# A one-core decoder layer: the scatter of finished rows behind the turn of the probabilities, and a prologue with x by partition, small weights first and aggregations inside the scale chains

## The chip, the cores and the metric

The kernel runs on one core of one Trainium2 chip. The metric is the device time of one execution in microseconds (us). A core has a matmul engine (TensorE, PE in the rows), a vector engine (VectorE, DVE), an activation engine (ScalarE, ACT), a general engine (GpSimd, POOL) and a queue engine for transfers (SyncE, SP). Each engine works through its own instructions in the order in which they are written; semaphores tie the engines together.

## The reference

x is 128 sequences of 64 tokens of 128 numbers; ctx has the same shape. Three residual blocks follow one another:

```
x = x + attention(layernorm(x))                 # 16 heads of 8, one key and value head
x = x + xattn(layernorm(x), ctx)                # a recurrence over the 64 tokens
x = x + ffn(layernorm(x))                       # 8 experts, top 1, 128 -> 512 -> 128

def step(carry, x_t):                           # xattn, for all 128 sequences
    h0, c0 = lstm_cell(concat(x_t, a), h0, c0, Wi0, Wh0, bi0, bh0)
    h1, c1 = lstm_cell(h0, h1, c1, Wi1, Wh1, bi1, bh1)
    attn  = softmax(einsum('bh,bsh->bs', h1 @ Wq.T, context))
    mixed = einsum('bs,bsh->bh', attn, context)
    a     = tanh(concat(mixed, h1) @ Wo.T + bo)
```

The outputs a of the recurrence are the second block's outputs. Each of its 64 steps needs the one before.

## The kernel before

The program has four stages, each a block with code of its own for every engine.

**Prologue** (lines 175 to 380). x is loaded in 8 chunks and ctx in 4 (SP's queue), the weights by ACT's queue. DVE takes the statistics of 64 token tiles of x (`bn_stats`, L293), aggregates them (`bn_aggr`, L296), takes the largest magnitudes of the weights and of ctx (L300 to L317) and makes scales that are powers of two from them (L319 to L343; the last of them releases `v_scale`). Numbers are kept as a high and a low 16-bit part: ACT makes the high parts of the 20 blocks of LSTM weights (`WL`, L212), and ACT and DVE the two parts of the projected context (`KH`, `VH`, L219 to L372) from TensorE's products (L278, L283), in 16 chunks through two buffers each (c % 2), so that chunk c waits until DVE has taken chunk c - 2. POOL makes the LSTM's bias rows (L254 to L262).

**Self-attention** (L483 to L775). 64 token tiles pass through a software pipeline, step i for tile i. Its result is `yv` (L756, DVE). POOL normalises tiles (L522, L528), adds `yv` to x (L534), and in steps 2 to 11 makes the low parts of the LSTM weights (`weight_rest`, L489 and L492, two blocks a step), which only the recurrence reads.

**Recurrence** (L985 to L1475). The 128 sequences are two groups of 64, a (G[0]) and b (G[1]), that run half a step apart. `half(L, A, ...)` is half a step: group L is in its LSTM cells while group A is in its cross-attention. It is called with L = a, A = b (the odd half) and then with L = b, A = a (the even half). The chain through one half on engine A's side is: scores (PE L1076) of the new hidden state, masked by DVE into `sm` (L1427), row maximum `nm` (L1433), exponent (ACT L1167), normalised probabilities `pe` (DVE L1444), their transpose by TensorE, the turn (L1108, semaphore `s_pt`), their two halves `pmv` (DVE L1454, L1456), the mixing matmuls `mx` (PE L1126), their sum `ar` (L1467), tanh on ACT (L1194) and the two parts of the new output `a_a` or `a_b` (DVE L1471, L1473). On L's side stand two LSTM cells: gates on PE (L1003), `gt` on ACT, `u`, `c` and `h` on DVE (L1393 to L1413).

Beside it runs a side line for tokens that are finished: `add_x1` (residual, L1334), statistics (L1339, L1343), `rstd` (POOL, L1246 to L1255), `normalise` (DVE L1350, writes `XN`), `copy_xn` (POOL L1281, L1282, into the row in `TOK`), router logits and the choice of an expert, `place` (POOL L1261 to L1268, a row's place) and `scatter` (POOL L1275): an indirect DMA that writes 128 rows of 258 numbers into `sorted_x` at the places in `slot`. One scatter stands in each odd half from step 4 on: 60 of them, and four more behind the last step. `TOK` has four slots, so that `add_x1` of token t waits for the landing of the scatter of token t - 4. What POOL runs in an odd half is written so:

```
if odd == 1 and live(t - 4):
    place(t - 4, (m - 4) % SLOTS)
    scatter(t - 4, (m - 4) % SLOTS)
if L:
    pool.tensor_copy(L.xs[:, :, :], XTn(L, lt + 1)).then_inc(L.s_xs, 1)
if odd == 1 and live(t - 1):
    rstd(t - 1)
```

**Experts** (from L1540): tiles of 128 sorted rows are read back, go through their expert's two layers and are scattered to the output.

## Time and profile before

| | |
|---|---|
| time, median of 3 runs | 1565.74 us (1564.30 to 1566.23) |
| time of the profiled execution | 1570.4 us |
| its span | 1568.7 us |
| prologue | 0 to 83 us |
| self-attention | 83 to 405 us |
| copying and start of the recurrence | 405 to 442 us |
| recurrence | 442 to 1377 us |
| tables, then experts | 1377 to 1398, then to 1568.7 us |
| busy: PE, DVE, ACT, POOL | 85%, 69%, 47%, 38% of the span |

The profile is of one execution. The rows that are shown further down give a start or a total in us, an engine, a line of the kernel, an operation with what it writes and reads, and in brackets how long the engine was idle ahead of it and what released it.

### The profile page before, as it was taken

The numbers are of one execution on the slowest core, as the hardware profiler recorded it, in microseconds if no ns is written. First come the engines' busy times: TensorE is split into PE (matmuls) and PEld (weight loads), VectorE is DVE, ScalarE is ACT, GpSimd is POOL, SyncE is SP. The second block draws the span as 40 slices with busy tenths as digits, with TensorE's granted clock in tenths as the row PEclk, the third lists the DMA queues.
The fourth block names the chain that finished last, engine by engine and source line by source line (L and its number), as shares of the span: only waits on it lengthen the run. The fifth ranks groups of instructions, "written<-read, shape, count | busy, mean of one in ns | idle before, by whom it ended". The sixth has DMA issues, their size and how long they took to land. (4 is left out here: it accounts for less than half of the span.)

```text
span 1568.7 us, 83724 instructions
## 1 busy us (share of the span) xinstructions
PE 1335.8 (85%) x34523; PEld 1195.8 (76%) x34523; DVE 1089.8 (69%) x4580; ACT 742.8 (47%) x2203; POOL 599.5 (38%) x1485
## 2 busy tenths in 40 slices
PE   0867888888499999999999999999999999839997
PEld 0556666666388888888888888888888888729996
DVE  7778999999456666666666666666666666636664
ACT  0656777787234444444444444444444444315553
POOL 1337555555402333333333333333333333224444
PEclk9979999999699999999999999999999999959999
DMA  8000000000320000000000000000000000022332
GB/s 255 1 2 16 17 17 17 17 17 17 110 53 11 19 16 18 19 16 18 19 16 18 19 16 18 19 16 18 19 16 18 19 16 18 14 82 80 95 96 56
DMA packets 49055, 52.62 MB, mean 34 GB/s; under 512 B 6026, under 2 KB 42252, under 8 KB 48168
## 3 DMA queue, kind: packets, MB, share of 16 engines
q1 hardware_dynamic: 41040, 32.50, 7.4%
q0 software_dynamic: 5344, 12.66, 2.3%
q8 instruction: 275, 4.51, 1.2%
q10 hardware_dynamic: 2296, 2.14, 0.4%
q14 instruction: 100, 0.82, 0.2%
HBM read 28.31 MB, written 19.42 MB: 30 GB/s over the span
## 5 line engine op out<-in xcount | busy, mean ns | idle before, releaser
L1076 PE MATMUL sc_ab<-h_a,KH 128*128 128x48 f16 (+2 forms) x4096 | 123.2, 183 | 2.2 <-DVE h_a L1413 2.2
L1076 PE MATMUL sc_ab<-h_b,KH 128*128 128x48 f16 (+2 forms) x4096 | 123.4, 183 | 0.3 <-issue 0.2
L1149 ACT ACTIVATE gt_a<-z_a,sc 128x256 f32<-128x256 f32 x128 | 60.6, 474 | 128.9 <-PE z_a L1003 128.9
L1126 PEld LDWEIGHTS mx_ab<-pmv_b,VH 128*128 128x128 f16 x4096 | 107.1, 96 | 16.3 <-DVE pmv_b L1456 16.3
L1126 PE MATMUL mx_ab<-pmv_b,VH 128*128 128x16 f16 x4096 | 113.0, 169 | 5.3 <-DVE pmv_b L1456 0.4
L1003 PE MATMUL z_a<-h_a,WL 128*128 128x64 f16 x2304 | 112.4, 193 | 5.6 <-DVE h_a L1405 2.0
L1003 PE MATMUL z_b<-h_b,WL 128*128 128x64 f16 x2304 | 112.0, 193 | 5.6 <-DVE h_b L1405 0.4
L1076 PEld LDWEIGHTS sc_ab<-h_a,KH 128*128 128x128 f16 x4096 | 113.1, 96 | 2.3 <-DVE h_a L1413 2.3
L1076 PEld LDWEIGHTS sc_ab<-h_b,KH 128*128 128x128 f16 x4096 | 113.3, 96 | 0.7 <-issue 0.5
L1126 PE MATMUL mx_ab<-pmv_a,VH 128*128 128x16 f16 x4096 | 112.2, 169 | 0.4 <-DVE pmv_a L1456 0.2
L1149 ACT ACTIVATE gt_b<-z_b,sc 128x256 f32<-128x256 f32 x128 | 60.6, 473 | 107.0 <-PE z_b L1003 107.0
L1589 POOL DMA_INDIRECT out<-ys,xr x71 | 70.2, 989 | 102.8 <-DVE ys L1689 80.0
L1126 PEld LDWEIGHTS mx_ab<-pmv_a,VH 128*128 128x128 f16 x4096 | 108.1, 96 | 1.0 <-DVE pmv_a L1456 1.0
L1261 POOL TENSOR_TENSOR w<-lr,one 128x8 f32<-128x8 f32 x60 | 12.1, 202 | 237.3 <-ACT lr L1189 237.3
L1003 PEld LDWEIGHTS z_a<-h_a,WL 128*128 128x128 f16 x2304 | 84.9, 97 | 19.8 <-DVE h_a L1413 10.4
L1650 ACT ACTIVATE hT<-psHa,b_sb 128x128 f32<-128x128 f32 x213 | 62.7, 365 | 75.0 <-PE psY L1622 38.9
L1003 PEld LDWEIGHTS z_b<-h_b,WL 128*128 128x128 f16 x2304 | 84.5, 97 | 17.4 <-DVE h_b L1413 12.9
L649 ACT ACTIVATE prT<-psT 128x512 f32<-128x512 f32 x128 | 69.9, 595 | 54.6 <-PE psT L585 54.6
L585 PE MATMUL psT<-ident,pr 128*128 128x128 f32 x512 | 73.5, 289 | 21.2 <-ACT pr L671 20.9
L1275 POOL DMA_INDIRECT sorted_x<-TOK,slot x64 | 70.1, 1096 | 51.1 <-DVE a_a L1473 44.9
L1160 ACT ACTIVATE tc_a<-c_a 128x64 f32<-128x64 f32 x128 | 32.8, 256 | 117.7 <-DVE c_a L1398 117.7
L1246 POOL TENSOR_SCALAR ve<-mvt 128x1 f32<-128x1 f32 x64 | 19.0, 297 | 174.1 <-DVE mvt L1343 174.1
(295 smaller groups left out, 3847.9 us busy)
## 6 DMA issues: line engine op xcount, KB each, us to landing
xr<-sorted_x SPq DMA_DIRECT2D x71, 129.0 KB
X<-in_x SPq DMA_DIRECT2D x8, 512.0 KB, 8.2
XT<-in_ctxT SPq DMA_DIRECT2D x4, 1024.0 KB
x_scratch<-X SPq DMA_DIRECT2D x8, 512.0 KB, 3.2
x1r<-x_scratch SPq DMA_DIRECT2D x64, 64.0 KB, 1.9
X<-in_w SPq DMA_DIRECT2D x1, 2048.0 KB, 9.0
sorted_x<-zt SPq DMA_DIRECT2D x12, 129.0 KB, 3.7
out<-ys,xr POOLq DMA_INDIRECT x71
```

The costliest lines, as they stand in the source:

```text
L585: mm = nc.tensor.transpose(psT[:, hp // 4, (hp % 4) * P:(hp % 4 + 1) * P], pr[:, u, 2 * hp:2 * hp + 2, :].rearrange("p h k -> p (h k)"), i ...
L649: nc.scalar.activation(prT[:, 4 * k:4 * k + 4, :].rearrange("p n t -> p (n t)"), psT[:, k, :], ACT.Copy).then_inc(a_pt, 1)
L1003: mm = nc.tensor.matmul(q.z[layer][:, j * GB:(j + 1) * GB], WL[:, blk + j, w, :], mov[m], start=False, stop=False, skip_group_check=True)
L1076: mm = nc.tensor.matmul(A.S[:, WIDE * n:WIDE * n + streamed(n)], KH[:, k, pair * P:(pair + 1) * P], A.h[1][:, 2 * n:2 * n + streamed(n) // ...
L1126: mm = nc.tensor.matmul(A.M[:, WIDE * n:WIDE * (n + 1)], VH[:, k, pair, :], A.pm[:, 2 * n:2 * n + WIDE // 2, :].rearrange("p b k -> p (b k)"),
L1149: nc.scalar.activation(L.gt[l][:, :, :].rearrange("p g b -> p (g b)"), L.z[l][:, 0:4 * GB], ACT.Tanh, scale=sc[:, I0 + l:I0 + l + 1]).then ...
L1160: nc.scalar.activation(L.tc[l][:, :], L.c[l][:, :], ACT.Tanh, scale=0.5).then_inc(L.s_tc[l], 1)
L1246: pool.tensor_scalar(ve[:, :], mv[:, 1:2], EPS, None, ALU.add).then_inc(g_r, 1)
L1261: pool.tensor_tensor(w8[:, :], lr[:, 1, :], one[:, :], ALU.mult).then_inc(g_pl, 1)
L1275: pool.indirect_dma_start(xs_dram, bass.IndirectOffsetOnAxis(slot[:, u:u + 1], 0), TOK[:, u, :], None).then_inc(d_sc[u], 16)
L1589: pool.indirect_dma_start(out_rows, bass.IndirectOffsetOnAxis(xr[:, u, AT_ROW:].bitcast(U32), 0), ys[:, u % 4, :], None, bounds_check=last ...
L1650: ins = nc.scalar.activation(hT[:, u, c, :], psHa[:, u, c * P:(c + 1) * P], ACT.Relu, bias=b1_sb[:, bass.ds(e * FC + c, 1)])
```

## The change

It has three parts.

**In the recurrence**, POOL's scatter moves behind the copy `xs` of the same odd half and gets one more wait, for the turn of group b's probabilities (`s_pt`). The wait is TensorE's transpose L1108. DVE's `normalise` moves from the even half's start to a place behind the second cell's `c`. `place` stays where it was.

**In the prologue**, x comes as `xP`, laid out on the host so that each partition reads 4 KB in one piece for a chunk and not 512 B rows; ACT's queue issues the six small weight loads ahead of the LSTM weights and biases; masks are made first on DVE; half of the 64 aggregations stand between the statistics and the other half inside two scale chains (`meanwhile`); the first chain covers the weights alone and releases ACT's `WL` copies and POOL's biases (`v_scale_w`), the second ctx (`v_scale`); the square root and the reciprocal of the statistics are done in two halves, the second of them, `WO2`'s low part and `smask` at the prologue's end.

**The low parts of the LSTM weights** (`weight_rest`) move from the attention steps 2 to 11 to the end of POOL's prologue.

```
 # recurrence, POOL
                         if odd == 1 and live(t - 4):
                             if not isinstance(t, int) or t < T:
                                 place(t - 4, (m - 4) % SLOTS)
-                            scatter(t - 4, (m - 4) % SLOTS)
                         if L:
                             if not (isinstance(lt, int) and lt == T - 1):
 
                                 ready(L.s_ah, 2 * lt)
                                 pool.wait_ge(L.s_xu, lt + 1)
                                 pool.tensor_copy(L.xs[:, :, :], XTn(L, lt + 1)).then_inc(L.s_xs, 1)
+                        if odd == 1 and live(t - 4):
+                            if A:
+                                pool.wait_ge(A.s_pt, at + 1)
+                            scatter(t - 4, (m - 4) % SLOTS)
 # recurrence, DVE
                         if odd == 0:
-                            if live(t - 2):
-                                normalise(t - 2, (m - 2) % SLOTS)
                             if live(t - 4):
                                 gate(t - 4, (m - 4) % SLOTS)
...
                         if L:
                             cell(1)
+                        if odd == 0 and live(t - 2):
+                            normalise(t - 2, (m - 2) % SLOTS)
 # self-attention, POOL
                     def step(i, u):
-                        if 2 <= i < 12:
-                            weight_rest(2 * i - 4)
-                            weight_rest(2 * i - 3)
 # prologue, POOL
-                    pool.wait_ge(v_scale, 1)
+                    pool.wait_ge(v_scale_w, 1)
...
+                    for blk in range(20):
+                        col = (S0 if blk < 12 else S1) + (8 if blk % 4 == 2 else 0)
+                        pool.wait_ge(a_w, blk + 1)
+                        if blk > 0:
+                            pool.wait_ge(g_wl, 2 * blk)
+                        pool.tensor_scalar(wlt[:, :], wl32[:, blk * P:(blk + 1) * P], sc[:, col:col + 1], None,
+                                           ALU.mult).then_inc(g_wl, 1)
+                        pool.wait_ge(g_wl, 2 * blk + 1)
+                        pool.tensor_tensor(WL[:, blk, 1, :], wlt[:, :], WL[:, blk, 0, :], ALU.subtract).then_inc(g_wl, 1)
 # prologue, SP
-                        sync.dma_start(Xp[:, k * nx:(k + 1) * nx, :], xw[:, k * nx:(k + 1) * nx, :]).then_inc(s_x[k], 16)
+                        cols = slice(k * nx * D, (k + 1) * nx * D)
+                        sync.dma_start(X[:, cols], xP[:, cols]).then_inc(s_x[k], 16)
 # prologue, ACT
-                    act.wait_ge(v_scale, 1)
+                    act.wait_ge(v_scale_w, 1)
                     for blk in range(20):
                         col = (S0 if blk < 12 else S1) + (8 if blk % 4 == 2 else 0)
                         nc.scalar.activation(WL[:, blk, 0, :], wl32[:, blk * P:(blk + 1) * P], ACT.Copy,
                                              scale=sc[:, col:col + 1]).then_inc(a_w, 1)
+                    act.wait_ge(v_scale, 1)
 # prologue, DVE (the new order)
+                    for k in range(XCH):
+                        dve.wait_ge(s_x[k], 16)
+                        for n in range(k * nx, (k + 1) * nx):
+                            nc.vector.bn_stats(st6[:, n, :], Xp[:, n, :]).then_inc(v_st, 1)
+                        if k < XCH // 2:
+                            for n in range(k * nx, (k + 1) * nx):
+                                aggregate(n)
+                    variance(0)
...
+                    def spread(k):
+
+                        meanwhile(6)
+                        dve.wait_ge(p_sc, 2 * k + 1)
+                        nc.vector.tensor_reduce(mxr[:, :], psS[0:8, 0:P], AX.X, ALU.max).then_inc(v_rd, 1)
+                        dve.wait_ge(v_rd, 2 * k + 1)
+                        nc.vector.tensor_scalar(dg[:, :], ident[0:8, 0:8], mxr[:, 0:1], None, ALU.mult).then_inc(v_rd, 1)
+                        meanwhile(5)
+                        dve.wait_ge(p_sc, 2 * k + 2)
+                        step(nc.vector.tensor_scalar(gm[:, :], psS[:, 128:136], 1e-12, 1e12, ALU.max, ALU.min))
+                    spread(0)
```

On POOL, in the odd half of a step in the middle of the recurrence, the order before is this (`slot` and `acc` end `place`; the DMA is the scatter; `ve` begins `rstd`):

```order
L1267 TENSOR_SCALAR slot<-w2s 128x1
L1268 TENSOR_TENSOR acc<-acc,one 128x8
L1275 DMA sorted_x<-TOK,slot 67584x258
L1295 COPY xs_a<-XT 128x128
L1246 TENSOR_SCALAR ve<-mvt 128x1
L1248 TENSOR_TENSOR yr<-ve,mhalf 128x1
```

and after the change the same place reads:

```order
L1309 TENSOR_SCALAR slot<-w2s 128x1
L1310 TENSOR_TENSOR acc<-acc,one 128x8
L1336 COPY xs_a<-XT 128x128
L1317 DMA sorted_x<-TOK,slot 67584x258
L1288 TENSOR_SCALAR ve<-mvt 128x1
L1290 TENSOR_TENSOR yr<-ve,mhalf 128x1
```

The scatter and the copy have changed places, and `rstd` now stands directly behind the scatter. On DVE, where an odd half ends and an even half begins, before:

```order
L1467 TENSOR_REDUCE ar_b<-mx_ab 128x64
L1471 TENSOR_SCALAR a_b<-a 128x64
L1473 SCALAR_TENSOR_TENSOR a_b<-a,a_b 128x64
L1350 TENSOR_SCALAR XN<-TOK,mvt,rst 128x128
L1385 RECIPROCAL TOK<-smt 128x1
L1427 TENSOR_TENSOR sm_a<-sc_ab,smask 128x128
```

and after the change, at the second cell of the even half:

```order
L1438 SCALAR_TENSOR_TENSOR u_b<-gt_b,c_b 128x64
L1440 SCALAR_TENSOR_TENSOR u_b<-gt_b 128x64
L1443 SCALAR_TENSOR_TENSOR c_b<-u_b 128x64
L1395 TENSOR_SCALAR XN<-TOK,mvt,rst 128x128
L1450 TENSOR_TENSOR h_b<-os_b,tc_b 128x64
```

`XN`, the normalised row, has moved from behind `a_b` to between `c_b` and `h_b` of the same even half.

## Rows read from the trace of the kernel before

**Rows 1.** Waits of VectorE in the recurrence, 500 to 1300 us: total us, times, longest

```profile
DVE sm_b L1427 <- PE sc_ab L1076: 71.7, 55, 1.4
```

**Rows 2.** Timeline of one odd half with a scatter: start us, us, engine, line, operation

```profile
999.03 0.23 DVE L1473 SCALAR_TENSOR_TENSOR a_a<-a,a_a 128x64 f16<-128x64 f32 x1
...
999.45 0.55 PE L1076 MATMUL sc_ab<-h_b,KH 128*128 128x48 f16 x16
...
999.97 0.52 PE L1003 MATMUL z_b<-h_b,WL 128*128 128x64 f16 x12
...
999.54 1.10 POOL L1275 DMA_INDIRECT sorted_x<-TOK,slot  x1 [0.76 <-DVE a_a L1473]
...
1000.92 0.29 DVE L1427 TENSOR_TENSOR sm_b<-sc_ab,smask 128x128 f32<-128x128 f32 x1 [1.33 <-PE sc_ab L1076]
...
1006.83 0.23 DVE L1473 SCALAR_TENSOR_TENSOR a_b<-a,a_b 128x64 f16<-128x64 f32 x1
...
1013.80 0.23 DVE L1473 SCALAR_TENSOR_TENSOR a_a<-a,a_a 128x64 f16<-128x64 f32 x1
```

**Rows 3.** Timeline of VectorE, an odd half of the first steps, without a scatter

```profile
485.38 0.29 DVE L1427 TENSOR_TENSOR sm_b<-sc_ab,smask 128x128 f32<-128x128 f32 x1 [0.45 <-PE sc_ab L1076]
```

**Rows 4.** Timeline, the rest of that odd half: turn, mixing, rstd, next even half

```profile
1003.06 0.33 PE L1108 MATMUL sc_ab<-ident,pe_b 128*128 128x128 f32 x1
...
1003.99 1.76 PE L1126 MATMUL mx_ab<-pmv_b,VH 128*128 128x16 f16 x64
...
1005.79 0.29 DVE L1467 TENSOR_REDUCE ar_b<-mx_ab 128x64 f32<-128x128 f32 x1 [0.40 <-PE mx_ab L1126]
...
1006.26 0.19 POOL L1255 TENSOR_TENSOR rst<-yr,yu 128x1 f32<-128x1 f32 x1 [0.18 <-POOL yu L1253]
...
1009.88 0.28 DVE L1334 TENSOR_TENSOR TOK<-psE,x1r 128x128 f32<-128x128 f32 x1
...
1011.72 0.24 DVE L1405 TENSOR_TENSOR h_b<-os_b,tc_b 128x64 f16<-128x64 f32 x1 [0.32 <-ACT tc_b L1160]
```

**Rows 5.** DMA issues, 1000 to 1100 us: count, median us from issue to landing

```profile
sorted_x<-TOK,slot POOLq DMA_INDIRECT x7, 2.8
```

**Rows 6.** Timeline of VectorE, self-attention: yv of steps 5, 11 and 31

```profile
129.03 0.29 DVE L756 TENSOR_TENSOR yv<-psSc,rden 128x128 f32<-128x128 f32 x1
...
165.19 0.29 DVE L756 TENSOR_TENSOR yv<-psSc,rden 128x128 f32<-128x128 f32 x1
...
257.97 0.29 DVE L756 TENSOR_TENSOR yv<-psSc,rden 128x128 f32<-128x128 f32 x1
```

**Rows 7.** Groups of instructions of GpSimd, 83 to 200 us: busy us, mean ns

```profile
L489 POOL TENSOR_SCALAR wlt<-wl,sc 128x128 f32<-128x128 f32 x20 | 12.1, 603 | 1.0
...
L492 POOL TENSOR_TENSOR WL<-wlt,WL 128x128 f16<-128x128 f32 x20 | 8.5, 427 | 1.7
```

**Rows 8.** Timeline of VectorE in the prologue

```profile
24.60 4.30 DVE L296 BATCH_NORM_AGGREGATE mv<-st 128x2 f32<-128x6 f32 x64
...
45.30 0.17 DVE L343 TENSOR_SCALAR sc<-sc 128x2 f32<-128x2 f32 x1
...
51.78 0.87 DVE L363 SCALAR_TENSOR_TENSOR WO<-wo_sb,sc,WO 128x128 f16<-128x128 f32 x1 [4.57 <-ACT WO L214]
```

**Rows 9.** Timeline of ScalarE, TensorE and GpSimd in the prologue

```profile
45.51 5.95 ACT L212 ACTIVATE WL<-wl,sc 128x128 f16<-128x128 f32 x20 [16.09 <-DVE sc L343]
...
43.39 2.08 PE L278 MATMUL psA<-XT,xwq_sb 128*128 128x512 f32 x2
...
53.37 2.08 PE L278 MATMUL psA<-XT,xwq_sb 128*128 128x512 f32 x2 [3.83 <-DVE KH L368]
...
59.49 1.02 PE L278 MATMUL psA<-XT,xwq_sb 128*128 128x512 f32 x2
...
61.24 1.02 PE L278 MATMUL psA<-XT,xwq_sb 128*128 128x512 f32 x2
...
58.06 1.03 POOL L260 COPY BL<-bhi 1x1024 bf16<-1x1024 bf16 x1
```

More of the change, by code:

```diff
@@ L1 @@
+import itertools
 from contextlib import ExitStack
@@ L224, in _ @@
                                              scale=sc[:, SV:SV + 1]).then_inc(a_v, 1)
+                    act.wait_ge(v_sd, 2)
+                    nc.scalar.activation(sd[:, hp:], sd[:, hp:], ACT.Sqrt).then_inc(a_sd, 1)
                 @block.gpsimd
@@ L267, in _ @@
                     pe.wait_ge(s_const, 8)
-                    pe.wait_ge(v_mx, 8 + CCH)
-                    nc.tensor.transpose(psS[0:8, 0:P], mx[:, :], ident[:, :]).then_inc(p_sc, 1)
-                    pe.wait_ge(v_sc, 2)
-                    nc.tensor.matmul(psS[:, 128:136], ones[0:8, :], dg[:, :], start=True, stop=True).then_inc(p_sc, 1)
+                    for k, m in enumerate((mx, mxb)):
+                        pe.wait_ge(v_mx, (7, 8 + CCH)[k])
+                        wait(pe, v_scale_w, k)
+                        nc.tensor.transpose(psS[0:8, 0:P], m[:, :], ident[:, :]).then_inc(p_sc, 1)
+                        pe.wait_ge(v_rd, 2 * k + 2)
+                        nc.tensor.matmul(psS[:, 128:136], ones[0:8, :], dg[:, :], start=True, stop=True).then_inc(p_sc, 1)
                     pe.wait_ge(s_wo, 96)
@@ L289, in _ @@
                 def _(dve):
-                    for n in range(NPAIR):
-                        if n % (NPAIR // XCH) == 0:
-                            dve.wait_ge(s_x[n // (NPAIR // XCH)], 16)
-                        nc.vector.bn_stats(st6[:, n, :], Xp[:, n, :]).then_inc(v_st, 1)
-                    for n in range(NPAIR):
-                        dve.wait_ge(v_st, n + 1)
-                        nc.vector.bn_aggr(mv[:, n, :], st6[:, n, :]).then_inc(v_st, 1)
-                    dve.wait_ge(v_st, 2 * NPAIR)
@@ L311, in _, with meanwhile, step @@
                                                 apply_absolute_value=True).then_inc(v_mx, 1)
+                    n = 0
+                    rest = iter(range(hp, NPAIR))
+                    def meanwhile(count):
+                        for pair in itertools.islice(rest, count):
+                            aggregate(pair)
+                    def step(ins):
+                        nonlocal n
+                        n += 1
+                        ins.then_inc(v_sc, 1)
+                        meanwhile(1)
+                        dve.wait_ge(v_sc, n)
+                    def spread(k):
[8 more added lines that the diff above has]
+                    spread(0)
+                    step(nc.vector.tensor_scalar(pw[:, :].bitcast(I32), gm[:, :].bitcast(I32), 0x7F800000, None,
+                                                 ALU.bitwise_and))
+                    step(nc.vector.tensor_scalar(tmp[:, 0:2], pw[:, 0:2], 2.0 ** -13, None, ALU.mult))
+                    step(nc.vector.reciprocal(sc[:, 0:2], tmp[:, 0:2]))
+                    step(nc.vector.tensor_scalar(sc[:, 8:10], sc[:, 0:2], 2.0, None, ALU.mult))
+                    nc.vector.tensor_scalar(sc[:, 4:6], tmp[:, 0:2], 0.5 / S, None, ALU.mult).then_inc(v_scale_w, 1)
                     for k in range(CCH):
@@ L366, in _ @@
+                    step(nc.vector.tensor_tensor(tmpb[:, 1:2], tmpb[:, 5:6], pw[:, 3:4], ALU.mult))
+                    step(nc.vector.reciprocal(sc[:, 2:4], tmpb[:, 0:2]))
+                    nc.vector.tensor_scalar(sc[:, 6:8], tmpb[:, 0:2], 1.0 / S, None, ALU.mult).then_inc(v_scale, 1)
+                    dve.wait_ge(a_sd, 1)
+                    nc.vector.reciprocal(rs[:, 0:hp], sd[:, 0:hp]).then_inc(v_rs, 1)
+                    meanwhile(hp)
+                    variance(1)
                     for c in range(16):
@@ L375, in _ @@
                             ALU.mult, ALU.subtract).then_inc(v_v, 1)
+                    dve.wait_ge(a_w, 21)
+                    nc.vector.scalar_tensor_tensor(WO2[:, 1, :], wo_sb[:, 1, :], sc[:, SV:SV + 1], WO2[:, 0, :],
+                                                   ALU.mult, ALU.subtract).then_inc(v_w, 1)
+                    dve.wait_ge(v_pm, 1)
+                    dve.wait_ge(v_scale, 1)
+                    nc.vector.tensor_scalar(
+                        smask[:, :].rearrange("p (n h k) -> p n h k", h=2, k=2),
+                        pm[:, :].unsqueeze(1).unsqueeze(3).broadcast_to([P, GP, 2, 2]),
+                        sc[:, IK:IK + 1], None, ALU.mult).then_inc(v_b, 1)
+                    dve.wait_ge(a_sd, 2)
+                    nc.vector.reciprocal(rs[:, hp:], sd[:, hp:]).then_inc(v_rs, 1)
         clear_semaphores()
```

102 lines of the change are left out of this document (42 added, 60 removed).

## The prediction

> **What bounds the kernel now.** I read three views. The waits of VectorE come first, over 800 us of the recurrence, since that stage is 935 of the 1568.7 us. One line stands out: the mask of group b, `sm_b`, waits 1.3 us at a time for the scores, 71.7 us in 55 waits [rows 1]. The timeline says why that is odd. The scores' last matmuls end at 999.45 + 0.55 = 1000.00, yet `sm_b` starts at 1000.92 [rows 2]; in the first steps, where no token is finished and no scatter runs, the same wait is 0.45 [rows 3]. What lies between is POOL's scatter, 999.54 to 1000.64, and `sm_b` comes 0.28 behind its end. TensorE itself isn't stopped, since its next matmuls run at 999.97 [rows 2]. So the result of a matmul that ends while the scatter runs reaches the engine that waits for it only about 1.38 after the scatter's start (1000.92 - 999.54). The chain of one half passes through this wait: `a_a` 999.03 to `a_b` 1006.83 is 7.80, and the even half without a scatter, to `a_a` at 1013.80, is 6.97 [rows 2]. Difference 0.83, in 60 halves 49.8 us. The longest rows of POOL in self-attention [rows 7] and the prologue's rows [rows 8, 9] give the other two stages.
>
> **The recurrence.** Removed: the scatter beside the scores of b, 60 x 0.83 = **-49.8 us**. Whether it comes back depends on what is awaited from TensorE at the new place. The scatter is now released by the turn, which ends at 1003.06 + 0.33 = 1003.39 [rows 4]. Its row starts some time behind its release; in the present place 0.76 behind POOL's last operation [rows 2]. I take 0.9, since the new release is a semaphore from another engine, so a start at 1004.3 and an end at 1005.4. By the 1.38 the results are held until 1005.68. The result awaited next from TensorE is the mixing product: its matmuls end at 1003.99 + 1.76 = 1005.75, and `ar_b` starts at 1005.79 [rows 4]. The hold is over 0.1 before. It is thin, so I put +0.05 a half, 60 x 0.05 = **+3.0 us**, with bounds of 0 and of the whole 0.83 (49.8 us) if the hold returns.
>
> What else moves with it: behind the scatter in POOL's queue stands `rstd`, six small operations that end at 1006.26 + 0.19 [rows 4]. It waits for the scatter now and ends some 1.6 later, at 1008.1. Its only reader is `normalise`, which therefore would be late at its old place (directly behind `a_b`, 1006.83) and is moved to about 1011.4, where `h_b` waits 0.32 for ACT anyway [rows 4]. A 128x128 operation of some 0.3 fits there: cost 0, at most 0.1 x 60 = 6 us if not. The gain of its removal behind `a_b` is nothing, since `sm_a` waits for the scores there. The scatter's landing, 2.8 after issue [rows 5], now comes at 1004.3 + 2.8 = 1007.1; it must be there for `add_x1` at 1009.88 [rows 4]. The copy `xs` ahead of it comes 1.1 earlier and is awaited by nobody sooner. Recurrence in sum: -49.8 + 3.0 = **-46.8**.
>
> **The Trainium skill against this reading.** The rows show a wait for TensorE that is 0.9 longer with a scatter than without [rows 1, 3]. The Trainium skill (SBUF — State Buffer, section Who interferes with whom) says that "PE and ACT never wait on anyone" and that only the port pair shared by VectorE and GpSimd is contended. By it no result of TensorE could be held, the 0.83 would belong to VectorE's own operations beside a GpSimd instruction and would travel with the scatter; the sum would be that of the rival "it travels" below.
>
> **Self-attention.** `yv` takes 36.16 us from step 5 to step 11 (129.03 to 165.19), and from step 11 to step 31 92.78 us, 4.64 a step [rows 6]. Six steps at 4.64 are 27.8, so the six are 8.3 too long. They are among those in which POOL makes the low parts, 20 pairs of 0.60 + 0.43 us, 20.6 busy [rows 7], most of them in this stretch. With these gone the steps should fall to 4.64. I take **-8.1** (a remainder of a step in its filling), bounds -8.3 and -6.5 (if part of it is a slower clock while the pipeline fills).
>
> **The prologue.** Ahead of the scales now: aggregations 4.30 us in one piece [rows 8], behind statistics that wait for x. With half of them in the load's gaps, half in the chains' gaps, and x in 4 KB pieces, the statistics end at about 22.2 rather than 28.9 (the end of the aggregations, 24.60 + 4.30), so -6.7. A second chain adds about +2.8 (two round trips to TensorE and some six small operations). The scale for ctx, written at 45.30 [rows 8], comes at 45.5 - 3.9 = 41.6. More is gained behind it: ACT makes the 20 weight blocks first, 5.95 us from 45.51 [rows 9], and only then begins on KH, so that TensorE, having filled both buffers, waits 3.83 and begins chunk 2 at 53.37 with matmuls at half speed (2.08 against 1.02 for the same two) [rows 9]. After the change those blocks are done while DVE is in ctx. TensorE starts chunk 0 about 3.8 earlier (43.39 to 39.6) at half speed, some 6.2 for two chunks, and goes on without a pause, each chunk 61.24 - 59.49 = 1.75 [rows 9]: chunk 2 at 46.0, chunk 4 at 49.6 against 59.49, so **-9.8**. Twelve chunks follow at the same rate. At the end DVE has `WO2`'s low part (0.87, [rows 8]), `smask` and a reciprocal that stood earlier; part of it lies behind chunk 15: **+0.9**, bounds 0 and 2. Sum **-8.9**, bounds -5 (x no faster, the aggregations still in the way) and -11.
>
> The low parts cost nothing there as long as POOL is ready first. Its biases took from 45.5 to 59.1 (58.06 + 1.03 [rows 9]), 13.6. They begin at about 29.1 now and end at 42.7; 20 pairs of 1.03 and gaps, 1.22 each, are 24.4, so 67.1. The prologue ends at about 83 - 8.9 = 74: cover 7 us.
>
> **Sum.** -46.8 - 8.1 - 8.9 = -63.8. The profiled execution took 1570.4 (span 1568.7), 4.7 above the median. It would take 1506.6; of the median of 1565.7 it leaves **1501.9**.
>
> **The rivals.**
>
> *The hold catches the mixing product in part.* For it: only 0.1 lies between. If the scatter's row starts 0.3 to 0.7 later than 1004.3 (the lag behind a semaphore is not shown in the middle of the chain), results come free at 1006.0 to 1006.4, `ar_b` is 0.2 to 0.6 late, and 60 x 0.4 = 24 us of the gain go: about 1523. Chance 0.16.
>
> *It travels.* Every scatter costs its half about 0.83 wherever it stands, as contention of VectorE or as a hold that reaches whatever is next. Against it: TensorE's end and the late `sm_b` [rows 2]. At the new place h_a's operations on VectorE would be drawn out, or `ar_b`. Then only prologue and attention remain: 1565.7 - 17.0 = 1548.7. Chance 0.09.
>
> *Slower.* The scatter's start falls at the mixing product's end: then `ar_b` waits the whole 1.38, more than the 0.83 removed. The point at which this outweighs everything is a new hold of (49.8 + 17.0) / 60 = 1.11 a half, that is a scatter that starts behind 1005.79 + 1.11 - 1.38 = 1005.5, 1.2 later than I put it, and ahead of 1005.75. At 1005.7 the hold is 1.29: 77.4 us, and 1565.7 - 17.0 + 77.4 - 49.8 = 1576.3. Chance 0.03.
>
> *POOL ends the prologue.* If the biases and low parts are drawn out by over 7 us, each further us is one. Doubling the pairs' 24.4 would cost 17: 1519. Against it: their durations beside a busy VectorE are in rows 7 already. Chance 0.03.
>
> **How the numbers follow.** The forecast as summed 0.67, its own range 1494 to 1509 (prologue -11 to -5, attention to -6.5, residue 0 to 0.1 a half). In part 0.16, it travels 0.09, POOL last 0.03, slower 0.03, no change 0.02. The range for 8 in 10 reaches from 1492 into the partial case, 1526. Within 0.2% (3 us, about what a measurement tells from no change) needs the gains of prologue and attention to be eaten: 0.02. Faster 0.95, slower 0.03.
>
> **What would show it.** In the changed trace: halves of 6.95 to 7.05 in both parities; `sm_b` waits of 0.45; the scatter's row at about 0.9 behind the turn's end, and the wait of `ar_b` still near 0.40. `normalise` between `c_b` and `h_b` without moving `h_b`. `yv` every 4.64 from the start. The prologue's end at 74, chunk 4 at 49.6, POOL's last low part at 67. The prediction is wrong if the wait of `ar_b` grows beyond 0.5, if `h_a` is late in halves with a scatter, or if DVE still waits for x at 25.

## The result, and the profile after

The changed kernel took 1547.49 us (median of 4 runs, 1544.14 to 1549.10) against 1565.99 for the kernel before on the same chip: a ratio of 0.987, 95% interval 0.985 to 0.989. It is faster, by 18.5 us, where 63.8 were forecast. The profiled execution has a span of 1546.9 us, 21.8 under that of before. By stage, from the traces: self-attention begins at 80.7 instead of 83.1 (-2.5), its steps 5 to 11 give -8.4, the recurrence's first `a_a` comes at 429.34 instead of 442.71 (-13.4 in all up to there), the recurrence from that `a_a` to the last `a_b` takes 925.99 instead of 933.28 (-7.3), and what follows -1.1. Of the 13.4, 2.5 that nobody forecast lie in the other attention steps and in the recurrence's start.

So self-attention did what was forecast, the prologue gave about a quarter of its 8.9, and the recurrence 7.3 of 46.8. These are VectorE's waits in the recurrence, 500 to 1300 us, after the change (total us, times, longest):

```profile
DVE sm_a L1470 <- PE sc_ab L1118: 53.6, 55, 1.8
DVE ar_b L1512 <- PE mx_ab L1168: 39.7, 55, 0.8
...
DVE sm_b L1470 <- PE sc_ab L1118: 25.3, 55, 0.7
```

The wait of `sm_b`, 71.7 in [rows 1], is down to 25.3, as forecast. In its place `ar_b` waits 0.7 for the mixing product at each scatter, and `sm_a`, in the half behind it, up to 1.8. In most even halves `sm_a` itself isn't late (it starts 1.01 behind `a_b` as before); VectorE only waits longer there, since `XN` no longer runs ahead of it. The timeline of one odd half with a scatter shows the first of these:

```profile
1024.77 0.23 DVE L1518 SCALAR_TENSOR_TENSOR a_a<-a,a_a 128x64 f16<-128x64 f32 x1
...
1027.94 0.33 PE L1150 MATMUL sc_ab<-ident,pe_b 128*128 128x128 f32 x1
...
1028.87 1.34 PE L1168 MATMUL mx_ab<-pmv_b,VH 128*128 128x16 f16 x47
...
1029.14 1.09 POOL L1317 DMA_INDIRECT sorted_x<-TOK,slot  x1 [3.54 <-DVE mvt L1388]
...
1030.42 0.59 PE L1168 MATMUL mx_ab<-pmv_b,VH 128*128 128x16 f16 x17 [0.21 <-issue]
...
1031.05 0.29 DVE L1512 TENSOR_REDUCE ar_b<-mx_ab 128x64 f32<-128x128 f32 x1 [0.70 <-PE mx_ab L1168]
...
1032.11 0.23 DVE L1518 SCALAR_TENSOR_TENSOR a_b<-a,a_b 128x64 f16<-128x64 f32 x1
```

The scatter starts 0.87 behind the turn's end (1028.27) and 4.37 behind `a_a`, where it was expected. The mixing matmuls, one piece of 64 in [rows 4], are in two: TensorE stops after 47 of them and goes on at 1030.42, 1.28 behind the scatter's start, and the row names no engine that it waited for ("issue"). The half takes 7.34 instead of 7.80. In all 60 odd halves with a scatter the mixing takes 2.06 to 2.25, where it took 1.76 to 1.87 before, and 59 show such a pause; their median is 7.35, in sum 442.0 us against 466.8, so -24.8.

The even halves took most of it back. 48 of 63 are 6.94 to 7.00 as before, but 15 take 8.05 to 8.21, together +17.5 us. One of them begins at 1046.43, and this is TensorE's clock in stretches of 0.4 us around it (the column behind the busy times is the granted clock; the first row holds the end of the pause, the last one the end of the slow stretch), then the scores in it:

```profile
1044.40:1044.80 0.40, 0.17 (x7) 0.08 (x4) 0.23 (x1) 0.04 (x1) 0.32 (x2) 1.00 0.00 0
1044.80:1045.20 0.40, 0.40 (x18) 0.40 (x18) 0.00 (x0) 0.00 (x0) 0.22 (x2) 0.81 0.27 103
1045.20:1045.60 0.40, 0.40 (x16) 0.40 (x14) 0.23 (x1) 0.00 (x0) 0.40 (x1) 0.50 0.64 228
...
1048.40:1048.80 0.40, 0.40 (x19) 0.40 (x16) 0.28 (x2) 0.28 (x2) 0.00 (x0) 0.92 0.00 0
```

```profile
1045.19 2.08 PE L1118 MATMUL sc_ab<-h_a,KH 128*128 128x48 f16 x48
```

The clock falls to its lower level (0.50, 1.2 GHz) about 0.3 us behind the pause in the mixing matmuls and stays there until 1048.4; the 48 score matmuls take 2.08, against 1.36 at full clock in the half of 1030.87. In the trace of before no even half is long.

The prologue after the change, on VectorE:

```profile
20.21 0.15 DVE L334 TENSOR_SCALAR sd<-mv 128x32 f32<-128x32 f32 x1
27.97 1.75 DVE L346 TENSOR_REDUCE mx<-wl 128x1 f32<-128x1536 f32 x1 [7.61 <-DMA wl<-in_wh1T]
...
44.39 1.71 DVE L378 TENSOR_SCALAR dg<-ident,mxr 8x8 f32<-8x8 f32 x1
```

and on GpSimd and TensorE:

```profile
43.96 2.12 POOL L275 TENSOR_TENSOR bw<-bw,bhi 128x1024 f32<-128x1024 f32 x1
...
52.76 1.02 PE L302 MATMUL psA<-XT,xwq_sb 128*128 128x512 f32 x2
```

The statistics are done at 20.3, earlier than the 22.2 of the forecast. But VectorE then waits 7.61 us for the LSTM weights. Chunk 2 starts at 52.76 against 53.37 [rows 9] and against 46.0 forecast; its clock is the full one, as forecast. A second loss is in `dg`, an 8x8 operation of 0.22 us elsewhere that took 1.71 and ended at 46.10, just behind POOL's operation (43.96 + 2.12 = 46.08). The Trainium skill (SBUF — State Buffer, section Who interferes with whom) has this: a `tensor_scalar` can use the port pair that VectorE shares with GpSimd, and the later one then waits for the whole of the other's instruction. The trace agrees: `dg` started second, at 44.39, and ended with the other.

Self-attention, `yv` of steps 5, 11 and 31:

```profile
126.19 0.29 DVE L798 TENSOR_TENSOR yv<-psSc,rden 128x128 f32<-128x128 f32 x1
...
153.93 0.29 DVE L798 TENSOR_TENSOR yv<-psSc,rden 128x128 f32<-128x128 f32 x1
...
246.74 0.29 DVE L798 TENSOR_TENSOR yv<-psSc,rden 128x128 f32<-128x128 f32 x1
```

Steps 5 to 11 take 27.74, against 36.16 in [rows 6]: -8.4, forecast -8.1.

### The profile page after: what moved, and what is told of

It is laid out like the page before. It is cut to its first block and busy times, and to the rows that moved or that the text cites. A ratio compares the mean times of both kernels' runs of the same rounds, so it can differ in the third digit from the quotient of the medians.

```text
span 1546.9 us, 83762 instructions
## 1 busy us (share of the span) xinstructions
PE 1345.5 (87%) x34526; PEld 1209.5 (78%) x34526; DVE 1102.6 (71%) x4589; ACT 744.3 (48%) x2204; POOL 594.7 (38%) x1485
## 5 line engine op out<-in xcount | busy, mean ns | idle before, releaser
L1168 PE MATMUL mx_ab<-pmv_b,VH 128*128 128x16 f16 x4096 | 122.5, 170 | 19.4 <-issue 14.1
L1168 PEld LDWEIGHTS mx_ab<-pmv_b,VH 128*128 128x128 f16 x4096 | 111.4, 96 | 35.7 <-issue 19.2
L1118 PE MATMUL sc_ab<-h_a,KH 128*128 128x48 f16 (+2 forms) x4096 | 136.2, 189 | 2.2 <-DVE h_a L1458 2.2
L1118 PEld LDWEIGHTS sc_ab<-h_a,KH 128*128 128x128 f16 x4096 | 126.2, 101 | 2.3 <-DVE h_a L1458 2.3
L1323 POOL COPY TOK<-XN 128x128 f32<-128x128 f32 x64 | 18.7, 293 | 260.4 <-DVE XN L1395 260.4
L627 PEld LDWEIGHTS psT<-ident,pr 128*128 128x128 f32 x512 | 55.6, 142 | 34.3 <-ACT pr L713 34.3
L789 DVE TENSOR_REDUCE pmx<-psSc 128x16 f32<-128x1024 f32 x64 | 78.4, 1224 | 3.3 <-PE psSc L618 2.4
```

The costliest lines, as they stand in the source:

```text
L627: mm = nc.tensor.transpose(psT[:, hp // 4, (hp % 4) * P:(hp % 4 + 1) * P], pr[:, u, 2 * hp:2 * hp + 2, :].rearrange("p h k -> p (h k)"), i ...
L789: nc.vector.tensor_reduce(mxv, sv, AX.X, ALU.max).then_inc(v_m, 1)
L1118: mm = nc.tensor.matmul(A.S[:, WIDE * n:WIDE * n + streamed(n)], KH[:, k, pair * P:(pair + 1) * P], A.h[1][:, 2 * n:2 * n + streamed(n) // ...
L1168: mm = nc.tensor.matmul(A.M[:, WIDE * n:WIDE * (n + 1)], VH[:, k, pair, :], A.pm[:, 2 * n:2 * n + WIDE // 2, :].rearrange("p b k -> p (b k)"),
```

## The experiments

The experiments fell on four chips, and the first thing that they showed is that chips are of two kinds. Two of the four behave like that of the result: a result of TensorE that falls due beside a scatter is held back from the engine that waits for it. This is called the hold below. The other two don't show it. The runs on each chip lie close together in time, so that it is the chip, and not something else that differed from one time to another, isn't shown. The kernel before's time on the same chip stands with each run.

| run | us | before on that chip | odd half | even half | long even halves |
|---|---|---|---|---|---|
| before (first chip) | 1565.99 | | 7.79 | 6.96 | 0 |
| changed (first chip) | 1547.49 | 1565.99 | 7.35 | 6.96 | 15 |
| scores_wait | 1508.76 | 1521.9 | 6.94 | 6.97 | 2 |
| no_wait | 1508.53 | 1521.9 | 6.94 | 6.96 | 2 |
| old_recurrence | 1510.24 | 1521.9 | 6.94 | 6.96 | 0 |
| lstm_first | 1512.37 | 1521.9 | 6.94 | 7.08 | 2 |
| changed_again | 1515.67 | 1520.24 | 6.94 | 7.08 | 1 |
| before_again | 1521.78 | 1520.24 | 6.95 | 6.96 | 0 |
| lstm_on_sync | 1502.67 | 1567.7 | 6.95 | 6.96 | 0 |
| low_in_attention | 1554.41 | 1567.7 | 7.36 | 6.96 | 10 |
| x_in_rows | 1550.37 | 1567.7 | 7.36 | 6.96 | 16 |
| pe_wait | 1517.51 | 1568.68 | 7.10 | 6.97 | 0 |
| pmv_wait | 1559.7 | 1568.68 | 7.55 | 6.99 | 12 |
| no_wait_2 | 1516.35 | 1568.68 | 6.98 | 6.96 | 1 |

Halves are medians over the steps with a scatter (odd) and over all steps (even), long ones are above 7.16, all in the profiled execution. The long ones of scores_wait, no_wait, lstm_first and changed_again are 7.2 to 7.4 at the full clock; those of the other runs are 7.9 to 8.2 and go with the lower one. pe_wait, pmv_wait, no_wait_2, low_in_attention, x_in_rows and before_again are one run each.

**The scatter's place, and the order of the loads.** scores_wait:

```
-                                pool.wait_ge(A.s_pt, at + 1)
+                                pool.wait_ge(A.s_sc, at + 1)
```

> Changed kernel, but the scatter waits for the scores of group b instead of for the turn of its probabilities. Theory (TensorE's results are held from about 0.16 to about 1.37 us behind the scatter's start, and TensorE itself stops if a long run of matmuls is under way): the scatter's row starts about 1.9 behind a_a, its hold falls between the row-maximum's matmul (1.83 behind a_a) and the gates of the second cell (3.24 behind a_a), so odd halves fall from 7.35 to 6.95 to 7.05, the pause in the mixing matmuls and with it the falls of TensorE's clock go, and the time is 1500 to 1510. Rival 1 (a scatter costs its half 0.4 or more wherever it stands): odd halves stay at 7.35 or more, 1545 or more. Rival 2 (the falls of the clock come from TensorE's greater load and not from its pause): odd halves near 7.0, but even halves of 8.1 as often as now or more often, 1520 to 1530.

no_wait leaves that wait out:

```
                         if odd == 1 and live(t - 4):
-                            if A:
-                                pool.wait_ge(A.s_pt, at + 1)
                             scatter(t - 4, (m - 4) % SLOTS)
```

> Changed kernel, the scatter behind the copy xs but without any wait for group b. Theory: it starts about 1.6 behind a_a (0.77 behind the end of the copy), so that its hold catches the row-maximum's matmul, which ends 1.83 behind a_a: nm_b is late by 0.3 to 1.1, odd halves of 7.3 to 8.0, 1525 to 1580. Rival (a scatter costs its half 0.4 wherever it stands): 7.35, 1545.

old_recurrence puts `scatter` back behind `place`, ahead of the copy, and `normalise` back to the even half's start:

```
                                 place(t - 4, (m - 4) % SLOTS)
+                            scatter(t - 4, (m - 4) % SLOTS)
...
-                        if odd == 1 and live(t - 4):
-                            if A:
-                                pool.wait_ge(A.s_pt, at + 1)
-                            scatter(t - 4, (m - 4) % SLOTS)
...
                         if odd == 0:
+                            if live(t - 2):
+                                normalise(t - 2, (m - 2) % SLOTS)
```

> Changed kernel with the recurrence as before (scatter ahead of the copy without a wait, normalise behind a_b); prologue and low parts as changed. Sum of the traces: the recurrence takes 7.3 us more than in the changed kernel, odd halves 7.79, even halves 6.96 without exception (no fall of TensorE's clock), 1553 to 1557. Rival (the falls of the clock come from the new prologue or its later phase, not from the scatter's place): even halves of 8.1 here too and 1565 or more.

lstm_first moves the six small loads behind the four of the LSTM weights:

```
-                    act.dma_start(xwq_sb[:, :], xwq).then_inc(s_wo, 16)
...
                     act.dma_start(w4[:, 4, :], wh1T).then_inc(s_w, 16)
 
+                    act.dma_start(xwq_sb[:, :], xwq).then_inc(s_wo, 16)
```

> Changed kernel, but the LSTM weights are issued ahead of the six small loads, as before; biases last. If VectorE's wait of 7.6 us for the LSTM weights at 20 to 28 us comes from their place in ScalarE's queue (3.5 us later), they land by about 12 and the prologue is 6 to 8 us shorter: 1540 to 1542. If it comes from the x and ctx loads, whose pieces are 4 and 8 KB against the weights' 2 KB in the same 16 engines, the weights still land at 24 to 28 and the time is within 3 us of 1547.

Ratios to before: scores_wait 0.992 (0.990 to 0.994), no_wait 0.991 (0.989 to 0.993), old_recurrence 0.992 (0.990 to 0.994), lstm_first 0.994 (0.992 to 0.995). These say nothing for or against the theory of the hold, since there is none on this chip: old_recurrence has its odd halves at 6.94 with the scatter where it always was, where 7.79 was expected, and took 1510.24 where 1553 to 1557 was expected. The times of scores_wait and no_wait look like a hit and a miss and are neither.

**Is it the chip?**

> The changed kernel as it is, since the four runs so far fell on a chip on which the kernel before takes 1521.9 instead of 1565.7 us and on which the odd halves of the recurrence take 6.94 with the scatter at the old place too. If the hold of TensorE's results belongs to the chip and not to the kernel: on the chip of the first runs 1547 with odd halves of 7.35 again; on the chip of the last four runs odd halves of 6.94 and, by the even halves of 7.08 that the same recurrence showed there with another order of loads, 1514 to 1517. Rival (the hold comes and goes from run to run on one chip): times of both kinds among the runs of one kernel here.

> The kernel before as it is, for its trace on this chip. If the hold belongs to the chip: odd halves of 7.79 and 1566 on the chip of the first runs; 6.94 and 1522 on that of the last four, with the mask of group b waiting 0.45 for the scores beside a running scatter.

They fell on another chip, of the same kind as that of the four runs above. The kernel before, one odd half beside a running scatter, on GpSimd and VectorE:

```profile
1000.59 1.10 POOL L1275 DMA_INDIRECT sorted_x<-TOK,slot  x1 [0.77 <-DVE a_a L1473]
...
1001.08 0.29 DVE L1427 TENSOR_TENSOR sm_b<-sc_ab,smask 128x128 f32<-128x128 f32 x1 [0.45 <-PE sc_ab L1076]
```

The same program, the same 1.10 us of scatter, and `sm_b` comes with the scatter 0.49 under way; on the first chip it came 0.28 behind its end [rows 2]. All times of one kernel on one chip were of one kind, so the rival of changed_again (the hold comes and goes from run to run) finds no support. What differs between the chips, no row tells. changed_again is also the changed program without the hold: its mixing is in one piece in every half, and the clock doesn't fall in its recurrence before the last steps. On this chip the change gives 0.9964 (0.9952 to 0.9976), and its recurrence is 7.4 us longer than before (891.7 against 884.4): even halves of 7.08 instead of 6.96. In the changed kernel here, GpSimd and VectorE at the start of an even half:

```profile
860.57 0.41 POOL L1336 COPY xs_b<-XT 128x128 f16<-128x128 f16 x1
...
860.63 0.43 DVE L1438 SCALAR_TENSOR_TENSOR u_b<-gt_b,c_b 128x64 f32<-128x64 f32 x1
```

and in scores_wait:

```profile
856.47 0.40 POOL L1336 COPY xs_b<-XT 128x128 f16<-128x128 f16 x1 [0.77 <-DVE a_b L1518]
...
857.29 0.21 DVE L1438 SCALAR_TENSOR_TENSOR u_b<-gt_b,c_b 128x64 f32<-128x64 f32 x1
```

With the scatter behind the turn, `rstd` ends so late that the copy `xs_b` queued behind it starts together with `u_b`, which then takes 0.43 instead of 0.21. An earlier scatter lets the copy start 0.4 behind `a_b`, and the half is 6.96. The copy was queued behind the moved scatter, and the prediction passed over it. The Trainium skill (SBUF — State Buffer, section Who interferes with whom) says that a VectorE instruction with two SBUF inputs contends with a GpSimd instruction that reads SBUF; `u_b` has two (`gt_b`, `c_b`), and the trace agrees, with 0.43 beside the copy and 0.21 apart from it.

**A chip with the hold: the scatter's place, and the loads again.** lstm_on_sync has the wait of scores_wait, and the LSTM weights in SyncE's queue between x and ctx:

```
                         sync.dma_start(X[:, cols], xP[:, cols]).then_inc(s_x[k], 16)
+                    w4 = wl32[:, :].rearrange("p (k n) -> p k n", n=4 * P)
+                    sync.dma_start(w4[:, 0:2, :], wi0T.rearrange("(a p) n -> p a n", a=2)).then_inc(s_w, 16)
...
-                                pool.wait_ge(A.s_pt, at + 1)
+                                pool.wait_ge(A.s_sc, at + 1)
```

> Changed kernel with two edits: the scatter waits for the scores of group b (as in scores_wait), and the four loads of LSTM weights stand in SyncE's queue between x and ctx instead of in ScalarE's. Theory of the loads (one queue's requests land in order and the weights in ScalarE's queue get a small share beside the larger pieces of x and ctx): the weights land right behind x, at 17 to 20 us, VectorE's wait of 7.6 to 8.4 us for them shrinks to under 1, and the prologue is 5 to 8 us shorter than in scores_wait. Rival (the prologue's end is then set by ctx or by the biases): the wait goes but the end moves by less than 2 us. On a chip without the hold 1500 to 1505 (1507 to 1510 if the rival holds); on one with the hold this run also shows the scatter's place: odd halves of 7.0 if the window between the row maximum's matmul and the second cell's gates is free, 7.35 or more if a scatter costs a half anywhere.

1502.67 us (1499.52 to 1504.38) against 1567.7: 0.958, interval 0.9565 to 0.9594. In the recurrence, an odd half that begins with `a_a` at 996.60 and ends with `a_b` at 1003.57:

```profile
998.46 1.09 POOL L1316 DMA_INDIRECT sorted_x<-TOK,slot  x1 [1.01 <-PE sc_ab L1117]
...
998.50 0.22 DVE L1475 TENSOR_REDUCE nm_b<-sc_ab 64x1 f32<-64x64 f32 x1
...
1000.72 1.76 PE L1167 MATMUL mx_ab<-pmv_b,VH 128*128 128x16 f16 x64
...
1002.52 0.29 DVE L1511 TENSOR_REDUCE ar_b<-mx_ab 128x64 f32<-128x128 f32 x1 [0.39 <-PE mx_ab L1167]
```

The scatter starts 1.86 behind `a_a`; the row maximum `nm_b` is already served, the mixing is in one piece, `ar_b` waits 0.39, and the recurrence takes 885.4 us where x_in_rows, with the changed kernel's recurrence on the same chip, takes 927.1. Both rivals fall: a scatter doesn't cost its half something wherever it stands, and TensorE's clock doesn't fall with greater load (PE is busy 784.3 of 800 us between 500 and 1300 us here and 772.4 in x_in_rows, and no even half is long). In the prologue VectorE's reduction of the LSTM weights starts at 20.30 without a wait and self-attention's first row on POOL at 71.98 instead of 80.66 (81.58 in scores_wait, so 9.6 where 5 to 8 were expected); the first `a_a` gains less, 424.83 against 429.34. Self-attention up to `yv` of step 5 takes 1.9 longer than in the changed kernel, and the recurrence's start 1.8; why is open.

low_in_attention makes the low parts in self-attention again:

```
                     def step(i, u):
+                        if 2 <= i < 12:
+                            weight_rest(2 * i - 4)
+                            weight_rest(2 * i - 3)
```

> Changed kernel with the low parts of the LSTM weights made in self-attention's steps 2 to 11 again. If they are the whole cause: yv from step 5 to step 11 takes 36.2 instead of 27.7 us, and the prologue, which ends with VectorE's work and not POOL's, stays as it is or gains up to 1 us from VectorE's operations that a POOL instruction drew out. Rival (the slower clock while the pipeline fills has a part): 28.5 to 35.

`yv` of its steps 5 and 11:

```profile
127.69 0.29 DVE L801 TENSOR_TENSOR yv<-psSc,rden 128x128 f32<-128x128 f32 x1
...
163.74 0.29 DVE L801 TENSOR_TENSOR yv<-psSc,rden 128x128 f32<-128x128 f32 x1
```

36.05 us, all but 0.1 of the 8.4 back: the low parts are the whole cause. Its prologue didn't gain the up to 1 us that was expected: self-attention begins at 81.95 against 80.66, mostly because the LSTM weights landed later: VectorE waited 8.48 for them instead of 7.61.

x_in_rows reads x as before:

```
-                        cols = slice(k * nx * D, (k + 1) * nx * D)
-                        sync.dma_start(X[:, cols], xP[:, cols]).then_inc(s_x[k], 16)
+                        sync.dma_start(Xp[:, k * nx:(k + 1) * nx, :], xw[:, k * nx:(k + 1) * nx, :]).then_inc(s_x[k], 16)
```

> Changed kernel with x read in rows of 512 B as before. Theory (the 16 transfer engines take pieces from the queues in turn, so the queue with the larger pieces gets the greater share): beside 512 B rows of x the LSTM weights land by 12 us as before, VectorE no longer waits for them at 20, but the statistics wait for x and end at 26 or later; the scales for the weights come no more than 3 us from where they come now. Rival (the weights are late because of their place in the queue alone): they land at 24 or later here too.

Its VectorE in the prologue:

```profile
16.72 1.65 DVE L339 BATCH_NORM_STATS2 st<-X 128x6 f32<-128x128 f32 x8 [3.68 <-DMA X<-in_x]
...
25.06 1.75 DVE L346 TENSOR_REDUCE mx<-wl 128x1 f32<-128x1536 f32 x1
```

The statistics end later (25.0 instead of 20.2), but the weights are there, and the weights' reduction starts 2.9 us *earlier* than in the changed kernel (25.06 against 27.97). By the updates of their semaphore in the traces, the last of the four loads of LSTM weights lands at 14.1 here and at 27.9 in the changed kernel, from the same place in ScalarE's queue. The rival (their place alone) would have had them at 24 or later. With lstm_first it is the other loads that come late:

```profile
20.35 1.74 DVE L346 TENSOR_REDUCE mx<-wl 128x1 f32<-128x1536 f32 x1
...
26.32 0.28 DVE L351 TENSOR_REDUCE mx<-xwq_sb 128x1 f32<-128x128 f32 x1 [3.10 <-DMA bo_sb<-in_bo]
```

With x in the larger pieces, whatever stands last in ScalarE's queue lands at 26 to 29, close to the end of all loading. The LSTM weights land at 10.0 in the kernel before, at 12.3 in lstm_first (their old place, large pieces), at 14.1 in x_in_rows (their new place, small pieces) and at 27.9 with both changed. So neither cause alone makes them late. lstm_first gained by it, but less than expected: its first `a_a` comes at 427.55, 3.7 us before that of changed_again, not 6 to 8.

**What ends the hold, what begins TensorE's stop.** Three waits for the scatter, on another chip with the hold. pe_wait and pmv_wait:

```
-                                pool.wait_ge(A.s_pt, at + 1)
+                                pool.wait_ge(A.s_pe, at + 1)        # pe_wait
+                                pool.wait_ge(A.s_pm, 2 * at + 2)    # pmv_wait
```

> Changed kernel, the scatter waits for the normalised probabilities pe_b on VectorE, 0.4 us ahead of the turn; for a chip on which results of TensorE are held. The scatter's row starts about 4.0 behind a_a instead of 4.37, the mixing matmuls at 4.10. Theory A (once results are held, TensorE goes on for a limited number of matmuls, about 0.94 us behind the scatter's start or 30 matmuls of mixing, and resumes 1.28 behind it): it stops after about 33 mixing matmuls, at 4.9, resumes at 5.28, the half is 7.1 to 7.4. Theory B (it stops at a fixed place in its program, after 47 mixing matmuls, because the next instructions are late): 47 matmuls and no pause or the same one, half 6.96 or 7.35. On a chip without the hold: 6.95.

> Changed kernel, the scatter waits for pmv_b, 0.5 to 0.6 us behind the turn; for a chip with the hold. Its row starts about 4.95 behind a_a, results are free at about 6.3. The mixing matmuls end ahead of TensorE's stop (0.94 behind the start is 5.89), but their result is held: ar_b starts at 6.3 instead of 5.9, odd halves 7.35 to 7.45, and TensorE pauses within the scores of a instead. If only TensorE's pause and not the held result had made the changed kernel's odd halves longer, they would be 6.96 to 7.1. On a chip without the hold: 6.95.

no_wait_2 is no_wait again:

> The kernel no_wait once more, for a chip with the hold. The scatter's row starts 1.30 behind a_a (as on the other chip), so results are held from 1.46 to about 2.65: the row maximum's matmul, which ends 1.83 behind a_a, reaches VectorE about 0.8 late and the odd half is 7.6 to 7.8. If the first release of 0.57 behind the start applies (1.87), the half is 7.0. If a scatter costs a fixed 0.4: 7.35. On a chip without the hold: 6.94.

pe_wait: the scatter starts 3.98 behind `a_a`, the mixing 0.12 behind it, and the half is 7.10. The mixing as a whole, then in stretches of 0.2 us (behind the stretch's length stand TensorE's busy time and, in brackets, its matmuls, which fall from 14 to 10 and 8; then its weight loads and VectorE's share; the clock is 1.00 throughout):

```profile
829.31 1.92 PE L1168 MATMUL mx_ab<-pmv_b,VH 128*128 128x16 f16 x64
```

```profile
830.10:830.30 0.20, 0.20 (x14) 0.20 (x12) 0.00 (x0) 1.00 0.00 0
830.30:830.50 0.20, 0.20 (x10) 0.15 (x7) 0.00 (x0) 1.00 0.35 82
830.50:830.70 0.20, 0.20 (x8) 0.18 (x7) 0.00 (x0) 1.00 0.00 0
830.70:830.90 0.20, 0.20 (x14) 0.20 (x12) 0.00 (x0) 1.00 0.32 124
```

It takes 1.92 instead of 1.76: a stall of 0.16 that ends 1.3 to 1.5 behind the scatter's start (829.19). A fixed place in TensorE's program (theory B) would have given no stall, or the changed kernel's, whose mixing takes 2.16 (median) instead of 1.76; it is not that. But by theory A TensorE would have stopped at 0.94. By the starts of the single matmuls in the halves shown, the last one ahead of the stop begins about 0.9 behind the scatter's start in the changed kernel and about 1.2 in pe_wait, some 35 and 42 matmuls behind it. So neither a time behind the scatter nor a number of matmuls sets where the stop begins; what does stays open. Its end is the fixed part, 1.26 to 1.36 behind the scatter's start.

pmv_wait: scatter 4.90 behind `a_a`, half 7.55, longer than the 7.35 to 7.45 expected. An odd half whose scatter starts at 849.88, on TensorE and VectorE:

```profile
849.08 1.76 PE L1168 MATMUL mx_ab<-pmv_b,VH 128*128 128x16 f16 x64
851.20 1.37 PE L1118 MATMUL sc_ab<-h_a,KH 128*128 128x48 f16 x48 [0.36 <-issue]
```

```profile
851.48 0.29 DVE L1512 TENSOR_REDUCE ar_b<-mx_ab 128x64 f32<-128x128 f32 x1 [0.94 <-PE mx_ab L1168]
```

The matmuls end at 850.84, unpaused; their result is served at 851.48, 0.64 later and 1.60 behind the scatter's start. TensorE pauses again, now ahead of the scores, and goes on 1.32 behind the start. So both effects are real: a result that falls due in the hold is late though TensorE has finished it, and TensorE stops in a long run of matmuls. Why this result came 1.60 and not 1.37 behind the start I can't say.

no_wait_2: scatter 1.30 behind `a_a`, and odd halves of two kinds, 6.94 to 7.01 in 50 of 60 and 7.7 or more in 8, so two of the three forecasts came true side by side. `nm_b` of a short one (`a_a` at 572.00, scatter at 573.30) and of a long one (`a_a` at 585.95, scatter at 587.25), with the row maximum's matmuls ahead of each:

```profile
573.39 0.45 PE L1135 MATMUL sc_ab<-II,sm_b 128*64 128x64 f32 x4
...
587.46 0.45 PE L1135 MATMUL sc_ab<-II,sm_b 128*64 128x64 f32 x4
```

```profile
573.93 0.22 DVE L1474 TENSOR_REDUCE nm_b<-sc_ab 64x1 f32<-64x64 f32 x1
...
588.62 0.22 DVE L1474 TENSOR_REDUCE nm_b<-sc_ab 64x1 f32<-64x64 f32 x1 [0.84 <-PE sc_ab L1135]
```

In the short one the matmul ends 0.54 behind the scatter's start and is served at 0.63; in the long one it ends at 0.66 and is served at 1.37. It is so in all but the last two odd halves: in 51 it ends up to 0.55 behind the start and is served within 0.1, in seven it ends at 0.61 to 0.79 and is served at 1.33 to 1.42. So a result that is 0.06 us later costs 0.75. But 0.6 is no general limit. In the kernel before the scores end 0.46 behind the scatter's start [rows 2], which is earlier, and are held until 1.38, and nearly all its halves are like that; only in three, where the scatter began 0.3 later, the scores ended at 0.15 and were served at 0.18 or 0.59. Where the hold begins depends on something that no run here isolates; where it ends, about 1.3 to 1.4 behind the start, is the same for both results.

## Why the prediction was wrong, step by step

**That results are held beside a scatter** was right for chips of the kind on which the result was measured, and moving the scatter away from the scores removed all of that wait: `sm_b` 0.45 where it was 1.33. **The 1.38** was nearly right too: TensorE resumes at 1.26 to 1.36, and a held result comes at 1.33 to 1.42 in no_wait_2, but at 1.60 in pmv_wait.

**The step that failed** is the one from there to the new place: "The hold is over 0.1 before", and ahead of it "TensorE itself isn't stopped, since its next matmuls run at 999.97". Those rows show TensorE at work only until 1000.49, which is 0.95 behind the scatter's start; then it had to wait for `sm_b` anyway, so a stop from there on could not have been seen. I read it as a rule. In the mixing, 64 matmuls long, TensorE does stop, and the 17 matmuls that are left when the hold ends make `ar_b` 0.39 late. The term "+0.05 a half" (3 us) was 0.39 and more a half: 442.0 us in the 60 odd halves against 60 x 6.96 = 417.6, **24.4 us**. The rival "in part" had this size (24 us) with another mechanism.

**What no rival had** is the clock. The pause is followed, in 15 of 60 cases, by a fall of TensorE's clock that costs 1.17 us each, **17.5 us**. The falls come and go with the pause: low_in_attention and x_in_rows, which have it too, have 10 and 16, pmv_wait with a pause of 0.36 has 12, and lstm_on_sync, changed_again and pe_wait with its 0.16 have none. The one exception is no_wait_2: one fall, behind a half in which the row maximum was held and the mixing was in one piece. So that this pause brings the falls is shown; why only in these 15 (three, four, eight or nine steps apart) is open. It is also open why the longer wait for `sm_b` in the kernel before, on TensorE's row for the row maximum, brought none:

```profile
1001.27 0.45 PE L1093 MATMUL sc_ab<-II,sm_b 128*64 128x64 f32 x4 [0.78 <-DVE sm_b L1427]
```

The odd halves gave 24.8 of the forecast 46.8, 22.0 too little; with these 17.5 that is all of the 39.5 us between forecast and measurement in the recurrence.

**The prologue** (-8.9 forecast, -2.5 measured): the statistics came earlier than forecast, "x in 4 KB pieces" was right. The step "a second chain adds about +2.8", which began the weights' reduction right behind the statistics, took for granted that the LSTM weights were there. They were issued 3.5 us later and beside larger pieces, and landed at 27.9 instead of 10.0: 7.6 us of waiting, and another 1.5 on `dg` behind POOL. The forecast's "if DVE still waits for x at 25" looked at the wrong transfer. lstm_on_sync, without that wait, has chunk 2 at 44.1 (forecast 46.0), chunk 4 at 47.6 (49.6) and self-attention at 72.0 (74), so the terms behind it (chunk 2 without a pause, at full clock) were right.

**Self-attention** (-8.1 forecast, -8.4 measured): right, and shown by low_in_attention. **POOL last in the prologue** did not happen: its last low part ends at 73.9, VectorE at 79.7.

**`normalise`** at its new place costs nothing: scores_wait and lstm_on_sync keep it there and have even halves of 6.96 to 6.97. **The copy behind `rstd`** cost nothing in the changed kernel on the first chip (6.96), and 0.12 a half on chips without the hold.

By the sentence of the Trainium skill (SBUF — State Buffer, section Who interferes with whom) that "PE and ACT never wait on anyone" no result would be held. On the chips without the hold the runs agree with it (`sm_b` waits 0.45 beside a running scatter), on those with it they don't (1.33); the measurement decides. What the rule would have given for the change, 1548.7, is within 2 us of the measured time, but by another way: the scatter's cost did not travel with it (lstm_on_sync is 1502.7 on a chip with the hold), it turned into a stop and a slower clock.

## What to carry to other kernels

When a long operation has to be moved away from a wait, look not only at which results fall due at its new place but at how much work the affected engine has in one run there: an engine that ran out of work by itself after 0.95 us in one place doesn't tell what it would do with more, and here it stopped after about that long. The gap between two results is only free if the run of instructions in it is short, and everything queued behind the moved operation (here `rstd` and a copy) moves too. When a queue's loads are made faster, check when the loads of the other queues land, since the engine will now be there earlier and they later. And measure a program that turns on such an effect on more than one chip.

## What the runs showed of the hardware

- Chips differ: one program took 1520 to 1522 us on two chips and 1566 to 1569 on the three chips met with the hold (the result's may be one of the other two), and its recurrence 884.4 and 933.3.
- Where there is a hold, a result of TensorE that fell due 0.61 to 0.79 us behind the start of GpSimd's indirect DMA row (1.1 us long) was served only at 1.33 to 1.42 (no_wait_2), and so was one that fell due at 0.46 in the kernel before, though one at 0.55 in no_wait_2 was not held. TensorE itself stops in a long run of matmuls (the last starts 0.8 to 1.2 behind the row's start) and resumes at 1.26 to 1.36.
- A pause of 0.2 to 0.4 us inside TensorE's work was followed by a granted clock of 0.50 in 10 to 16 of 60 cases (four traces), each costing the half behind it 1.1 to 1.2 us; a stall of 0.16 by none.
- An 8x8 `tensor_scalar` on VectorE took 1.71 us instead of 0.22 beside a 2.12 us operation of GpSimd.
